# Projections and counts of a fused attention kernel as two 64-row tiles in two crossed runs, in a new order

## The reference

```python
q = rms_norm(proj(Wq), qn_w); k = rms_norm(proj(Wk), kn_w); v = proj(Wv)   # 16 heads of 16
out = softmax(q @ k.T * scale) @ v                                        # per batch and head
attention = out @ Wo.T
...
scores = layer_norm(xn) @ centroids.T          # 8192 tokens, 8 experts
# each expert in turn takes the 1024 tokens not yet taken that score highest
h = gelu(layer_norm(routed) @ w1 + b1) @ w2 + b2
experts = routed + h                            # back in the tokens' order
```

## Time and profile before

| | us |
|---|---|
| median of 3 runs | 1061.7 (1061.24 to 1061.93) |
| the profiled execution's own time | 1061.36 |
| its span in the profile | 1059.6 |
| TensorE busy (matmuls) | 1028.2 |
| VectorE busy | 815.7 |
| ScalarE busy | 745.0 |
| GpSimd busy | 715.9 |
| first pair of heads starts at | 35.3 |

### The profile page before, as it was taken

One profiled execution on the slowest core, in us unless ns is written; L12 is line 12 of the kernel. 1 busy time (PEld: TensorE's weight loads), 2 busy tenths in 40 slices (PEclk: granted clock), 3 DMA queues, 4 the chain that ended last, 5 costly groups with the idle time before them and its releaser, 6 DMA issues.

```text
span 1059.6 us, 20747 instructions
## 1 busy us (share of the span) xinstructions
PE 1028.2 (97%) x7215; PEld 670.6 (63%) x7215; DVE 815.7 (77%) x1858; ACT 745.0 (70%) x966; POOL 715.9 (68%) x753
## 2 busy tenths in 40 slices
PE   5889999999999999999999999999999999999997
PEld 4445555554554454455454443698889999988997
DVE  8999896788788788778777785786777677687861
ACT  3678888888888888888888888755555545455540
POOL 5677878776767767677677657666557676765434
PEclk9999999999999999999999999999999999999999
DMA  4644744444443543533534446153434344452313
GB/s 150 206 153 140 236 161 163 146 155 139 161 148 132 184 148 119 202 128 131 190 121 150 169 161 234 37 147 51 127 53 112 86 90 103 83 126 49 66 21 40
DMA packets 83529, 138.18 MB, mean 130 GB/s; under 512 B 9808, under 2 KB 35792, under 8 KB 83408
## 3 DMA queue, kind: packets, MB, share of 16 engines
q1 hardware_dynamic: 54560, 103.09, 28.7%
q0 software_dynamic: 12288, 16.79, 9.6%
q10 hardware_dynamic: 16560, 16.78, 4.8%
HBM read 86.28 MB, written 50.33 MB: 129 GB/s over the span
## 4 chain that ended last, share of the span: by engine, by line
PE 88%; DVE 6%; issue 2%; ACT 2%; POOL 1%; POOLq 0%; ACTq 0%; DVEq 0%
PE pv L509 19%; PE W L1489 17%; PE S L1475 17%; PE S L494 14%; PE W L453 9%; PE W L478 5%; PE W L464 4%; DVE xb L789 2%; ACT prob L710 1%; PE R L423 1%; PE R L1461 1%; PE pv L1461 1%; DVE raw L844 1%; PE R L434 0%; PE R L552 0%
## 5 line engine op out<-in xcount | busy, mean ns | idle before, releaser
L710 ACT ACTIVATE prob<-S 128x1024 f32<-128x1024 f32 x512 | 496.3, 1023 | 90.0 <-PE S L494 88.8
L509 PE MATMUL pv<-prob,v 128*17 128x512 f32 x2048 | 246.7, 595 | 0.7 <-DVE oT L877 0.7
L494 PE MATMUL S<-stq,stk 64*128 64x512 f32 x1024 | 194.6, 452 | 4.9 <-ACT prob L710 3.3
L494 PEld LDWEIGHTS S<-stq,stk 64*128 64x128 f32 x1024 | 84.4, 184 | 126.8 <-ACT prob L710 107.4
L1752 POOL DMA_INDIRECT out<-prob,order_rows x64 | 105.7, 1651 | 52.4 <-DVE prob L1691 41.4
L509 PEld LDWEIGHTS pv<-prob,v 128*17 128x17 f32 x2048 | 46.0, 96 | 112.1 <-issue 111.3
L1551 ACT ACTIVATE wq_act<-S,b 128x512 f32<-128x512 f32 x64 | 43.9, 685 | 95.2 <-PE S L1475 94.8
L1214 POOL TENSOR_TENSOR sq<-raw 128x512 f32<-128x512 f32 x62 | 64.5, 1041 | 64.8 <-DVE raw L844 42.7
L1475 PE MATMUL S<-raw_nT,xT_w 128*128 128x512 f32 x384 | 91.1, 395 | 0.0
L1244 POOL TENSOR_TENSOR lo<-full,hi 128x512 fp32r<-128x512 f32 x62 | 80.5, 1298 | 5.0
L1475 PEld LDWEIGHTS S<-raw_nT,xT_w 128*128 128x128 f32 x384 | 71.6, 188 | 17.7 <-issue 1.7
(11 more groups left out here) (257 smaller groups left out, 2550.4 us busy)
## 6 DMA issues: line engine op xcount, KB each, us to landing
stk<-parts SPq DMA_DIRECT2D x93, 256.0 KB, 3.6
stq<-parts SPq DMA_DIRECT2D x93, 256.0 KB, 4.6
xT<-in_w SPq DMA_DIRECT2D x32, 512.0 KB, 4.8
parts<-hi SPq DMA_DIRECT2D x63, 256.0 KB, 2.1
parts<-lo SPq DMA_DIRECT2D x63, 256.0 KB, 2.1
out<-ao ACTq DMA_DIRECT2D x32, 256.0 KB, 2.6
xb<-in_x ACTq DMA_DIRECT2D x13, 512.0 KB, 4.6
xb<-in_x SPq DMA_DIRECT2D x2, 512.0 KB, 5.4
```

The source lines that it names most:

```text
L494: ins = e.matmul(S[n % 2][:, h, :], stack["k"][u][64 * h:64 * h + 64, p, c * P:(c + 1) * P], stack["q"][u][64 * h:64 * h + 64, p, :], star ...
L509: ins = e.matmul(pv[32 * j:32 * j + VW, :], v[b % 2][:, c, 8 * u + 4 * g + j, :], prob[(2 * t + j // 2) % RING][:, j % 2, :], start=(c == ...
L710: e.activation(prob[n % RING][:, :, :], S[n % 2][:, :, :], ACT.Exp).then_inc(s_exp, 1)
```

## The change

The two banks `W[0]` and `W[1]` become one tensor `Wb`, and `crossed` is the first half (256 columns) of both. A projection outside the set-up and the lean periods is done in 64-row tiles, each contributing half of the contraction, with 256 columns of the moving operand: in the first run the upper rows' tile writes bank 0 and the lower rows' tile bank 1, in the second run the other way round. A count is likewise split into two halves of rows. The order in a period becomes: pair, first run, pair, values, pair, lower half of the count, second run, pair, upper half of the count, values; then `score_x`, `order_tensor` and `turn_x`. A projection starts only when the one before it is drained, since it uses both banks. VectorE's `turn_raw` and `copy_v` move to the head of its list. `evict_o` keeps its place on ScalarE.

```diff
+def is_lean(at):
+    return at >= PERIODS * (B - 1) - 2
+def set_up(nb, i):
+    return nb == 0 or (nb == 1 and i < 2)
+def projected(at):
+    b, kk = divmod(at, PERIODS)
+    for m in (b + 1, b + 2):
+        for i in range(4):
+            if m < B and qk_at(m, i) == at and not set_up(m, i):
+                return "qk", m, i
+    for i in range(2):
+        if b + 1 < B and v_at(b + 1, i) == at:
+            return "v", b + 1, i
+    return ("o", b - 1, kk - 4) if b and kk in (4, 5) else None
+def projected_before(at):
+    return next((projected(t) for t in reversed(range(at)) if projected(t)), ("qk", 1, 1))
+def asked(at):
+    ex, i = routed(at)
+    return ex is not None and (ex < E - 1 or i == 0)
+def straight_by(at):
+    return sum(1 for t in range(at + 1) if projected(t) and not is_lean(t))
...
-    W = [ps(f"W{i}", [P, N]) for i in range(2)]
+    Wb = ps("W", [P, 2, N])
+    W = [Wb[:, i, :] for i in range(2)]
+    crossed = Wb[:, :, 0:D]
...
+    def row_tiles(e, operands, n, i, turn):
+        for j in range(6):
+            for h in range(2):
+                c = h ^ turn
+                ins = e.matmul(crossed[:, c, :], *operands(n, i, j, c, slice(64 * h, 64 * h + 64)),
+                               start=(j == 0 and turn == 0), stop=(j == 5 and turn == 1))
+        return ins
+    def wait_drained(e, kind, n, i):
+        if kind == "qk":
+            e.wait_ge(s_raw, 4 * n + turn_of(n, i) + 1)
+        elif kind == "v":
+            e.wait_ge(s_v, 2 * n + turn_of(n, i) + 1)
+        else:
+            e.wait_ge(s_ao, 2 * n + i + 1)
+    def start_projection(e, at):
+        kind, n, i = projected(at)
+        wait_drained(e, *projected_before(at))
+        if kind == "o":
+            e.wait_ge(s_onl, 2 * n + 2)
+            row_tiles(e, o_operands, n, i, 0).then_inc(s_straight, 1)
+        else:
+            e.wait_ge(s_xl, 2 * n + 2)
+            row_tiles(e, qk_operands if kind == "qk" else v_operands, n, i, 0).then_inc(s_straight, 1)
+    def end_projection(e, at):
+        kind, n, i = projected(at)
+        e.wait_ge(s_straight, straight_by(at))
...
-    def route_tensor(e, ex, i):
+    def route_tensor(e, ex, i, h):
+        def half(to, weights, moving, first):
+            r = slice(64 * h, 64 * h + 64)
+            return e.matmul(to, weights[r, :], moving[r, :], start=(h == 0 and first), stop=(h == 1),
+                            skip_group_check=True)
+        if h:
+            e.wait_ge(r_low, ROUNDS * ex + i + 1)
...
                 heads(e, b, 4 * kk)
+                straight = projected(at) and not lean
+                if straight:
+                    start_projection(e, at)
                 if not lean:
                     heads(e, b, 4 * kk + 1)
                 if at:
                     weigh(e, 2 * at - 2)
+                if not lean:
+                    heads(e, b, 4 * kk + 2)
+                    if asked(at):
+                        route_tensor(e, *routed(at), 0)
+                    if straight:
+                        end_projection(e, at)
+                    heads(e, b, 4 * kk + 3)
+                    if asked(at):
+                        route_tensor(e, *routed(at), 1)
                 if lean:
                     heads(e, b, 4 * kk + 1)
                     heads(e, b, 4 * kk + 2)
...
-                if not lean:
-                    heads(e, b, 4 * kk + 2)
-                heads(e, b, 4 * kk + 3)
...
-        e.activation(ao[i][:, :, :].rearrange("p c d -> p (c d)"), W[i][:, :], ACT.Copy).then_inc(s_ao, 1)
+        src = crossed if b < B - 2 else W[i].rearrange("p (c d) -> p c d", c=2)
+        e.activation(ao[i][:, :, :], src, ACT.Copy).then_inc(s_ao, 1)
...
+                for m in (nb, nb + 1):
+                    for i in range(4):
+                        if m < B and qk_at(m, i) + 1 == at:
+                            turn_raw(e, m, i)
+                for i in range(2):
+                    if nb < B and v_at(nb, i) + 1 == at:
+                        copy_v(e, nb, i)
                 ex, i = routed(at)
...
-                for m in (nb, nb + 1):
-                    for i in range(4):
-                        if m < B and qk_at(m, i) + 1 == at:
-                            turn_raw(e, m, i)
```

More of the change, by code:

```diff
@@ L469, in project_o @@
         e.wait_ge(s_onl, 2 * b + 2)
[L470 to L473, removed]
+        e.wait_ge(s_ao, 2 * (b - 1) + i + 1)
         for c in range(2):
@@ L480, in project_o, with qk_operands, v_operands, o_operands @@
         ins.then_inc(s_wo, 1)
+    def qk_operands(nb, i, j, c, r):
+        u, n, d, (pw, px) = i // 2, "qk"[i % 2], j // 3, PRODUCTS[j % 3]
+        return w[n][pw][r, d, u * P:(u + 1) * P], (xh, xl)[px][nb % 2][r, d, D * c:D * (c + 1)]
+    def v_operands(nb, i, j, c, r):
+        d, (px, pw), at = j // 3, PRODUCTS[j % 3], (2 * i + c) * P
+        return (xh, xl)[px][nb % 2][r, d, at:at + P], w["v"][pw][r, d, :]
+    def o_operands(b, i, j, c, r):
+        u, (px, pw), at = j // 3, PRODUCTS[j % 3], (2 * i + c) * P
+        return (onh, onl)[px][r, u, at:at + P], w["o"][pw][r, u, :]
+    def row_tiles(e, operands, n, i, turn):
[24 more added lines that the diff above has]
+        e.wait_ge(s_straight, straight_by(at))
+        if kind == "qk":
+            row_tiles(e, qk_operands, n, i, 1).then_inc(s_proj, 1)
+        elif kind == "v":
+            row_tiles(e, v_operands, n, i, 1).then_inc(s_vp, 1)
+        else:
+            row_tiles(e, o_operands, n, i, 1).then_inc(s_wo, 1)
     def heads(e, b, hs):
@@ L526, in shift_tensor @@
         e.wait_ge(g_in, 64 * (n + 1))
-    def route_tensor(e, ex, i):
-        if i == 0 and ex:
[L530 to L535, removed]
+    def route_tensor(e, ex, i, h):
[5 more added lines that the diff above has]
+            e.wait_ge(r_low, ROUNDS * ex + i + 1)
+        else:
+            if ex == E - 1:
+                e.wait_ge(r_last, 1)
+            elif i < STEPS:
+                e.wait_ge(r_pc, STEPS * ex + i + 1)
+            else:
+                e.wait_ge(r_ch, 3 * ex + 3)
+        if i == 0 and ex:
+            half(R[:, NT:2 * NT], below, sel, True)
+            ins = half(R[:, 2 * NT:3 * NT], ones_h, sel, False)
+            if h:
+                ins.then_inc(r_rank, 1)
@@ L536, in route_tensor @@
         if ex == E - 1:
-            e.matmul(R[:, 3 * NT:4 * NT], below[:, :], sel_last[:, :], start=True, stop=True)
-            e.matmul(R[:, 4 * NT:5 * NT], ones_h[:, :], sel_last[:, :], start=True, stop=True).then_inc(r_rank, 1)
+            half(R[:, 3 * NT:4 * NT], below, sel_last, False)
+            half(R[:, 4 * NT:5 * NT], ones_h, sel_last, False).then_inc(r_rank if h else r_low, 1)
         elif i < STEPS:
-            e.wait_ge(r_pc, STEPS * ex + i + 1)
-            e.matmul(R[:, 0:CANDS[i]], ones_h[:, :], part_cnt[:, 0:CANDS[i]], start=True, stop=True).then_inc(r_cnt, 1)
-        else:
[L543 to L546, removed]
+            ins = half(R[:, 0:CANDS[i]], ones_h, part_cnt[:, 0:CANDS[i]], not (i == 0 and ex))
@@ L548, in order_tensor @@
+            ins.then_inc(r_cnt if h else r_low, 1)
+        else:
+            half(R[:, 0:1], ones_h, gt_cnt, True)
+            half(R[:, NT:2 * NT], below, eq, False)
+            ins = half(R[:, 2 * NT:3 * NT], ones_h, eq, False)
+            ins.then_inc(r_tie if h else r_low, 1)
     def order_tensor(e, i):
@@ L615, in tensor_program @@
                     x["turn"](e, 0, 1)
-                if not lean:
-                    heads(e, b, 4 * kk + 2)
-                heads(e, b, 4 * kk + 3)
-                for m in (nb, nb + 1):
-                    for i in range(4):
[L621 to L627, removed]
+                if lean:
+                    heads(e, b, 4 * kk + 3)
+                    if projected(at):
+                        project_o(e, b - 1, kk - 4)
                 if scored(at - 1) is not None:
@@ L631, in tensor_program @@
                     turn_x(e, scored(at - 2), 1)
-                ex, i = routed(at)
-                if ex is not None and (ex < E - 1 or i == 0):
-                    route_tensor(e, ex, i)
         weigh(e, 16 * B - 2)
@@ L843, in turn_raw @@
             e.wait_ge(s_full, 2 * (2 * (nb - 1) + u) + 2)
-        e.transpose(raw[u][:, n, :], W[n][:, :]).then_inc(s_raw, 1)
+        if set_up(nb, i):
+            e.transpose(raw[u][:, n, :], W[n]).then_inc(s_raw, 1)
+        else:
+            e.transpose(raw[u][:, n, :].rearrange("p (c q) -> p c q", c=2), crossed).then_inc(s_raw, 1)
     def sum_squares(e, nb, u):
@@ L867, in copy_v @@
             e.wait_ge(s_pv, 16 * (nb - 1))
-        e.tensor_copy(v[nb % 2][:, 2 * i:2 * i + 2, :, 0:DH],
-                      W[i][:, :].rearrange("p (c h d) -> p c h d", c=2, h=H)).then_inc(s_v, 1)
+        src = W[i].rearrange("p (c h d) -> p c h d", c=2, h=H) if nb == 0 else crossed.rearrange("p c (h d) -> p c h d", h=H)
+        e.tensor_copy(v[nb % 2][:, 2 * i:2 * i + 2, :, 0:DH], src).then_inc(s_v, 1)
     def denominators(e, b, q):
```

(3 more changed lines are left out.)

7 lines of the change are left out of this document (2 added, 5 removed).

## The result

The changed kernel takes 1206.18 us (median of 4 runs, 1205.47 to 1209.33) against 1061.7; the ratio is 1.137, with a 95% interval of 1.1354 to 1.1381. That is 144.5 us slower, 24 more than forecast and inside the range. The profiled execution took 1209.33 us, of which 1207.6 are the span; it is the slowest of the four, 0.3% above their median.

The account below looks back on a forecast made before the run. TensorE, without idle time in the attention stage, was taken to bound the kernel, so its waits add to the end. 6 + 54 + 7 + 6 + 38 + 10 = 121 us on 1061.36 gave 1182 us, range 1120 to 1238.

Parts of the forecast that it names:

- (1): TensorE's work per period: 4.91 us against 4.84, row tiles saving nothing, dearer counts adding 6 us.
- rival B: Row-tile runs: weight loads don't hide behind matmuls of their own row group; 156 us more, 1339 us; 7%.
- the 6 us for the counts: Split counts between pair and run: an exposed load makes each dearer, 77 x 0.08 us in all.
- (2): Run waits for eviction: 1.58 us after kk 0, 2, 6, 0.41 after kk 4, 5; routed +54, late lists +7 us.
- Rival A: VectorE's evictions come in time, so only counts and transposes cost: 1073 us; 4%.
- The forecast for periods 32 to 109: Routed stage: eviction stalls +54 us, longer VectorE lists with some late counts +7, and the split counts' cost.
- (3): Scored periods (1 to 27 and 31): an extra change of shape at turn_x, +6 us, and eviction stalls, +38 us.
- The stall after even periods: Scored periods, before the first run: 1.58 us less the 0.69 that turn_x covers, 0.9 us.
- (4): Periods 110 to 117: ordering columns between denominators and eviction lengthen the stalls, +10 us.
- Rival C: Adjacent 64-row blocks make changes into and out of 17-column value tiles free: 64 us less over 118 periods; 3%.

Follow-up runs that it names:

- e1: The changed kernel with VectorE's denominators of even periods moved to the next period's list, behind evictions and answer: 1142.29 us, ratio 1.075.
- e5: The changed kernel with turn_raw moved back behind answer, ask and choose in VectorE's list: 1312.6 us, ratio 1.237.
- e8: The changed kernel's row tiles with both values together as before, and exponentials of only 384 of 512 columns (output not the reference's): 1055.95 us, ratio 0.993.
- e4: The changed kernel's row tiles, crossed runs and drained-first list, but in the old order with both values together: 1070.27 us, ratio 1.0072.

## Why the prediction was right

**The sum on TensorE** (1) was right in its result, and 0.09 too high: an undisturbed routed period is 4.82, not 4.91. Row tiles of 256 columns follow each other in 0.118, the loads of both tiles hidden, as taken; rival B would have given 0.22 and falls. The Trainium skill (TensorE: Matmul & The Clock Gate, section Part 3: Packing small matmuls) has a load overlap a running matmul only where its row group differs; this trace, with 0.118, doesn't agree. The term that was off is the lower half of the count, priced at 0.14 with an exposed load: it starts at 644.43 and the run behind it at 644.44, 0.34 after the pair, as without a count. So the 6 us for the counts were hardly paid: the 29 routed periods with kk 0, 2 and 4 grew by 2.5 us together.

**The wait for the drained banks** (2) happened as worked out: 1.77 from pair to run where 1.81 to the load was forecast, and e1 took this one order away and 64 us with it. Rival A falls. Of the 29 routed periods after kk 0, 2 and 6, 13 take 6.3 to 6.5 for the 6.49 forecast; the others take up to 8.6. Most of those after kk 4 and 5 take 5.27 to 5.38 for 5.3. The forecast for periods 32 to 109 was 67 with counts, measured 75 and 7 in period 32 alone. Period 32 was one mis-sized part. The eviction before its first run stood behind `keep_score`, which the late `score_x` held, and two transposes, and TensorE waited 2.27 us for it. Then VectorE splits the scores in five operations before the first question, and since a count's half now stands in mid-period, TensorE waited 2.24 for the question:

```profile
263.17 0.39 PE L535 MATMUL W<-xh,wq 64*128 64x256 f32 x2 [2.27 <-DVE raw L950]
...
268.97 0.19 PE L620 MATMUL R<-part_cnt,ones_h 64*128 64x7 bf16 x1 [2.24 <-DVE part_cnt L1053]
```

Another was overlooked: in 11 of the 29 periods an operation of `split_scores`, last in VectorE's list of the even period, also stands between `denominators` and the eviction (VectorE, batch 7, kk 3):

```profile
424.65 0.72 DVE L983 STREAM_TRANSPOSE oT<-pv 128x512 f32<-128x512 f32 x1 [3.31 <-PE pv L597]
...
425.58 0.74 DVE L1019 TENSOR_TENSOR xb<-xb,scores 128x64 int32<-128x64 int32 x1
426.25 0.68 DVE L975 COPY v<-W 128x512 f32<-128x512 f32 x1
```

There the run started 2.12 us late instead of 1.4; over the 11 periods that makes 4.7 us.

**The scored periods** (3): 44 forecast, 51.8 measured. The stall after even periods was right (97.76 - 96.58 - 0.34 = 0.84 for 0.9). After kk 1 it was 1.81 before the run instead of 2.3, but `turn_x` had already waited 0.53 for the bank. After kk 3 it was 1.77 for 1.85, after kk 7 only 1.28. **Ordering** (4): 10 forecast, 14.2 measured.

**What the sum left out** is TensorE's clock, and that is about as large as the missing 24 us. In kk 3 of batch 7 TensorE waited 1.96 us for the eviction, began again at 426.98, and ran at 1.2 GHz, half of its clock, from about 428.5, when it was busy throughout:

```profile
426.98 0.50 PE L535 MATMUL W<-wv,xh 64*128 64x256 f32 x4 [1.96 <-DVE v L975]
...
428.09 1.63 PE L597 MATMUL pv<-prob,v 128*17 128x512 f32 x8
```

The values took 1.63 us where they take 1.05 at full clock. Kk 7 of batch 11 had nearly the same wait, 1.93 us, and no fall. The windows view of both, each from the run's start to the next period's first pair, and of the slow part of the first:

```profile
426.98:433.11 6.13, 6.13 (x48) 3.35 (x48) 3.87 (x13) 2.91 (x3) 5.36 (x6) 0.72 0.30 109
428.50:431.00 2.50, 2.50 (x18) 1.25 (x12) 1.42 (x4) 1.24 (x2) 1.90 (x3) 0.50 0.15 50
...
637.15:641.74 4.59, 4.59 (x48) 2.45 (x49) 3.73 (x12) 2.92 (x3) 3.27 (x4) 1.00 0.16 58
```

The same 48 matmuls took 1.54 us more at a mean clock of 0.72, which withheld 0.28 x 6.13 = 1.72 us of full clock. Over the span the clock was 0.976 and before 0.999, so 29 us were withheld instead of 1. At the same rate that is about 25 us, an estimate. Half of TensorE's busy time in the stretches that the trace has at half clock gives about the same, 24 us, in the groups of the forecast 8 (scored), 3 (period 32), 7 (33 to 109) and 6 (ordering). Without them the groups would stand at 44, 4, 68 and 8.6, beside 44 forecast for the scored periods, 67 for periods 32 to 109 together and 10 for the ordering. No run held the clock at full speed, so the estimate isn't shown by an experiment; e1, with fewer waits, has a clock of 0.987 and e5, with longer ones, 0.947.

That the groups come out so close is in part luck: in the routed periods the 6 us of counts that weren't paid stand against 4.7 of `split_scores` and the excess of period 32, in the scored ones a shorter wait after kk 7 against 6.7 us of waits for bank `R`.

Rival C had its mechanism in the wrong place: no change of shape was free (the way out of values is 0.12 in both). Where the row tiles did save, in e8, the order has two changes of shape fewer; that this is what saved was argued in e4's sum and not tried by itself.

## What to carry to other kernels

When a block moves to the end of a period, list who waits for it, and what stands behind that waiter on its in-order engine: here one transpose behind the late values cost more than all the matmul tiling could save. Taking away double buffering makes the distance from a result's last write to the next one's first the new budget; fill it with other work on the same engine, put the eviction first in every list, and look at what the list of the period before ends with. And an engine at 99% may hide a loop of nearly the same length through another: shorten both, or neither gains. Where waits of microseconds come into a stage that had none, leave room in the forecast for the clock: here it took about a sixth of the loss, by the estimate above.

## What was not expected of the hardware

- Two 64-row tiles on different banks needn't run in step: a count in one of them alone adds nothing visible to the run that follows (644.43, and the next tile at 644.44). Behind another such run the two matmuls of the next pair, which start together elsewhere, start 0.13 apart:

```profile
418.29 0.39 PE L582 MATMUL S<-stq,stk 64*128 64x512 f32 x1
...
418.42 0.40 PE L582 MATMUL S<-stq,stk 64*128 64x512 f32 x1
```

- TensorE's clock fell to 1.2 GHz a microsecond and a half after it had gone back to work from a wait of 1.96 us. Waits of the same length did and didn't do it: one of 1.92 in batch 5, kk 7, was followed by a fall; one of 1.92 in batch 8 and one of 1.93 in batch 11, both kk 7, were not. Each fall compared made the wait dearer than its own length, by about 1.5 us. e5, whose waits are longest, has the lowest granted clock (0.947).
